# A graph attention kernel: statistics and gain of the output stage moved into layer 2's pass, and the input rows added on POOL

## Chip, cores and metric

The kernel runs on one core of one Trainium2 chip. The metric is device microseconds of one execution. Five engines work side by side, each on its own queue of instructions: TensorE (PE), VectorE (DVE), ScalarE (ACT), GpSimd (POOL) and SyncE (SP, which here only issues transfers). They meet at semaphores.

## What is computed

The input is a graph of 3125 nodes with 256 features each and 53125 edges, sorted by destination. Layer 0 normalises the rows, sums weighted neighbours in both directions and adds the means to x. Then two graph attention layers run over the same edges, layer 1 with 8 heads of 64 features, layer 2 (the output layer) with one head of 256. The stage around the change is the end of layer 2:

```
e = exp(-leaky_relu(s_src[src] + s_dst[dst]))
h_prime = segment_sum(e[:, None] * h[dst], src, num_segments=N)   # 3125 x 256
mu, var = mean(h_prime, axis=-1), var(h_prime, axis=-1)
h_prime = (h_prime - mu) * rsqrt(var + 1e-5) * g_out + beta_out
x = x + elu(h_prime)
```

Everything is float32.

## The kernel before

Nodes are tiled by 128 (T = 25 tiles). Edges were sorted by tile earlier in the kernel, each tile's edges are padded to groups of 256, and a group is two chunks of 128 edges. There are 232 groups, a bound that holds for any graph of this size, so 464 chunks, taken four at a time as 116 quads, numbered 0 to 115. The groups behind the last real edge are padding and belong to the last tile. `tiles_done(groups)` gives how many tiles are complete for sure after so many groups. `FIRST` is the first quad after which one is (103), and `BLOCKS` lists, for each quad from there on, the tiles which that quad is sure to complete: 13 blocks, tile 0 alone and then two tiles each.

One pass over the quads is `attend(o)`, with o = "2" for the output layer; the function stands once for each engine, and all loops are unrolled in Python, four quads a turn. For a quad q:

- POOL issues four gathers (L389, one indirect DMA for 128 rows of the table) into 16 slots; a slot is free again when PE has summed its chunk. Half of the slots lie in `rows_near`, half in `given`.
- ACT makes one-hot matrices (L568, L572), PE transposes them and looks up the source scores (L817, L827).
- DVE adds the two scores when the rows have landed (L1186) and takes leaky relu (L1190), ACT the exponential (L581), DVE the messages (L1199 for layer 2, four instructions), PE the sums of two groups in PSUM (L842, eight matmul records), and DVE adds each to its tile in `work` (L1040).

DVE's order in one turn is: messages of quad q, scores of q + 1, additions of q - 1. Each engine's queue is in program order, so an instruction that waits holds all behind it.

After the pass comes the output stage. DVE takes row statistics of 25 tiles (L1302), then their moments (L918), ACT one square root over all tiles (L652). Then a loop over tiles goes round three engines: DVE subtracts the mean and multiplies by g (L1308), ACT multiplies by 1/std (L657), POOL adds beta (L479), ACT takes relu(-y) and its exponential (L613, L615) and DVE finishes ELU (L1242) and adds x into one of four output slots (L1299). DVE runs six tiles behind itself: `finish(t - 6)` follows the product of tile t. SP writes each output slot to DRAM (L376). The one-hot, message and output buffers share a scratch area.

The blocks of layer 0 (`beside_rows` on DVE, L1144 on) do a like thing to what the change does: statistics of a block's tiles inside a pass.

Of the kernel before, what the change touches and what calls it, by code (L numbers as in the profile page):

```python
# [9 lines left out]
ALU = mybir.AluOpType  # L10
# [5 lines left out]
C = 256  # L16
# [3 lines left out]
HD = HEADS * D  # L20
# [31 lines left out]
def tiles_done(groups):  # L52
    return sum(1 for t in range(T) if (E + (t + 1) * (GROUP - 1)) // GROUP <= groups)
# [3 lines left out]
BLOCKS = [range(tiles_done(2 * q), tiles_done(2 * q + 2)) for q in range(FIRST, QUADS)]  # L57
SUMS0 = 6
assert tiles_done(GROUPS) == T and all(1 <= len(b) <= 2 for b in BLOCKS) and len(BLOCKS) < 16
assert CHUNKS % SLOTS == 0 and CHUNKS <= 512 and P * COLS >= E and FULL < P and COLS % BATCH == 0  # L60
assert SLOT_W <= 12 * HD and T % BLOCK == 0 and all(c % 2 == 0 for c in CUT)

def build(nc, x, src, dst, edge_weight, W_heads, b_heads, a_heads, g_heads, beta_heads,
          W_out, b_out, a_out, g_out, beta_out, out):
    ctx = ExitStack()
    with ctx:
# [37 lines left out]
        square = carve(0, 8, HD)  # L104
        neg_exp = carve(4 * HD, 2, HD)
        final = carve(6 * HD, 4, C)
# [197 lines left out]
        square_used = sem("square_used")  # L304
        scaled = sem("scaled")
        gained = sem("gained")
# [74 lines left out]
        def _(pool):  # L381
# [95 lines left out]
            for t in range(T):  # L477
                pool.wait_ge(scaled, t + 1)
                nc.gpsimd.tensor_tensor(work[:, t, 0:C], work[:, t, 0:C], betao[:, :], ALU.add).then_inc(offset_added, 1)  # L479

        @block.scalar
        def _(act):
# [123 lines left out]

            def elu_exponential(n, slot, y):

                e = neg_exp[:, slot, 0:y.shape[-1]]
                act.wait_ge(offset_added, n + 1)  # L610
                if n >= 2:
                    act.wait_ge(z_done, n - 1)
                nc.scalar.activation(e, y, ACT.Relu, scale=-1.0).then_inc(act_chain, 1)  # L613
                act.wait_ge(act_chain, n + 1)
                nc.scalar.activation(e, e, ACT.Exp, scale=-1.0).then_inc(exp_ready, 1)  # L615
# [34 lines left out]
            attend("2")  # L650
            act.wait_ge(moments_ready, 3 * T)
            nc.scalar.activation(rstd[:, :], mv[:, :, 1], ACT.Sqrt, bias=eps[:, :]).then_inc(std_ready, 1)  # L652
            act.wait_ge(nb_ready, 2 + len(BLOCKS))
            for t in range(T + 2):
                if t < T:
                    act.wait_ge(gained, t + 1)
                    nc.scalar.activation(work[:, t, 0:C], work[:, t, 0:C], ACT.Copy, scale=rstd[:, t:t + 1]).then_inc(scaled, 1)  # L657
                if t >= 2:
                    elu_exponential(t - 2, t % 2, work[:, t - 2, 0:C])

# [212 lines left out]
        def _(dve):  # L873
# [290 lines left out]
            for n in range(4):  # L1164
                beside_rows(QUADS + 2 + n)

            def attend(o):
                heads, width = (HEADS, HD) if o == "1" else (1, C)
# [42 lines left out]
                def turn(i):  # L1211

                    tiles = tile_numbers(mybir.EngineType.DVE, "S", i * (2 * UNROLL) + (TILE_AT - 2), 2 * UNROLL)
                    for u in range(UNROLL):
                        q, static = i * UNROLL + u, isinstance(i, int)
                        messages(q, u)
                        if not static or q + 1 < QUADS:
                            scores(i, i * UNROLL + (u + 1), u + 1)
                        if not static or q >= 1:
                            add_groups(i * UNROLL + (u - 1), u - 1, tiles[2 * u:2 * u + 2])  # L1220

                scores(0, 0, 0)
# [13 lines left out]
            def per_head(a):  # L1236
                return a.rearrange("p (h d) -> p h d", h=HEADS)

            def elu(n, slot, y):

                dve.wait_ge(exp_ready, n + 1)
                return v.scalar_tensor_tensor(out=y, in0=neg_exp[:, slot, 0:y.shape[-1]], scalar=-1.0, in1=y, op0=ALU.add, op1=ALU.max)  # L1242

# [48 lines left out]

            def finish(t):
                y = work[:, t, 0:C]
                elu(t, t % 2, y).then_inc(z_done, 1)
                dve.wait_ge(z_done, t + 1)
                if t >= 4:
                    dve.wait_ge(q_out[t % 4], 16 * (t // 4))
                v.tensor_tensor(final[:, t % 4, :], y, xs[:, t, :], ALU.add).then_inc(final_ready, 1)  # L1299

            for t in range(T):
                v.bn_stats(stats[:, t, :], work[:, t, 0:C]).then_inc(stats_ready, 1)  # L1302
            for t in range(T):
                tile_moments(t, 2 * T)
            dve.wait_ge(moments_ready, 3 * T)
            for t in range(T):

                v.scalar_tensor_tensor(out=work[:, t, 0:C], in0=work[:, t, 0:C], scalar=mv[:, t, 0:1], in1=go[:, :],  # L1308
                                       op0=ALU.subtract, op1=ALU.mult).then_inc(gained, 1)
                if t == 0:  # L1310
                    dve.wait_ge(std_ready, 2 + len(BLOCKS))
                    v.reciprocal(rstd[:, :], rstd[:, :]).then_inc(nb_ready, 1)
                if t >= 6:
                    finish(t - 6)
            for t in range(T - 6, T):
                finish(t)
# [21 lines left out]
```

## Time and profile before

| | us |
|---|---|
| median of 3 executions | 3050.62 |
| lowest, highest | 3050.2, 3058.38 |
| the profiled execution | 3054.22 |
| its span, first to last instruction | 3052.4 |
| DVE, PE, ACT, POOL busy in the span | 2157.3, 2332.0, 1582.3, 1967.1 |

The span is that of the profiled execution; times such as 2996.12 are microseconds from its start. A group line gives engine, source line, operation, output and inputs by tile names, and how many instructions it merges; in a timeline the first two numbers are the start and the length in us, and brackets at the end say how long the engine was idle before and for whom. The table of stretches lists, after the length of each stretch, busy us and count of PE matmuls, PE weight loads, DVE, ACT and POOL, then the granted clock of PE (1.00 would be 2.4 GHz, 0.50 is 1.2 GHz), the share of the transfer engines and GB/s. Shares of the whole span mix five stages with different limits, so the rows below are of single stretches. Layer 2's pass runs from about 2400 to 2996.5, the output stage behind it.

### The profile page before, as it was taken

How to read it: one execution, taken by the hardware profiler on the slowest of the kernel's cores; microseconds unless marked ns; L12 is line 12 of the kernel's file. 1: busy time of each engine (PE TensorE's matmuls, PEld its weight loads, DVE VectorE, ACT ScalarE, POOL GpSimd, SP SyncE). 2: the span in 40 equal slices, each digit the busy share in tenths (PEclk: the TensorE clock that was granted, in tenths of full speed). 3: DMA queues.
4: the chain of work that ended last, by engine and by line, in shares of the span. 5: the costliest groups of instructions: out<-in, count | busy, mean ns of one | idle time of the engine just before them, and what ended most of it. 6: DMA issues, size and time to landing. Idle time of an engine off the chain costs nothing. (4 is left out here: it accounts for less than half of the span.)

```text
span 3052.4 us, 48976 instructions
## 1 busy us (share of the span) xinstructions
PE 2332.0 (76%) x16450; PEld 1796.2 (59%) x16450; DVE 2157.3 (71%) x4448; ACT 1582.3 (52%) x4526; POOL 1967.1 (64%) x2003
## 2 busy tenths in 40 slices
PE   1787699989888899966677888888865677777771
PEld 1677698879887799843344444444434555555551
DVE  9999989988986799832244887888877344343437
ACT  0464467656765676633333555455539455555544
POOL 2000177777777777777773777777756477777772
PEclk7999899989998899955568999999987778777885
DMA  2001011111114322222254777777760233333352
GB/s 64 1 1 44 11 50 50 50 50 50 50 50 47 54 50 50 57 54 52 53 64 119 209 211 205 205 209 211 207 126 19 87 107 106 106 106 106 106 96 56
DMA packets 114891, 270.64 MB, mean 89 GB/s; under 512 B 34543, under 2 KB 51670, under 8 KB 114646
## 3 DMA queue, kind: packets, MB, share of 16 engines
q0 software_dynamic: 89088, 245.53, 32.7%
q1 hardware_dynamic: 25558, 21.98, 2.2%
q8 instruction: 137, 2.24, 0.3%
q14 instruction: 108, 0.88, 0.1%
HBM read 250.96 MB, written 16.42 MB: 88 GB/s over the span
## 5 line engine op out<-in xcount | busy, mean ns | idle before, releaser
L389 POOL DMA_INDIRECT rows_near<-table_a,s_idx_S x464 | 486.4, 1048 | 227.4 <-issue 111.5
L1040 DVE TENSOR_TENSOR work<-work,bank 128x129 f32 (+2 forms) x928 | 390.2, 420 | 288.7 <-PE bank L726 195.1
L389 POOL DMA_INDIRECT rows_near<-table,s_idx_S x464 | 450.0, 970 | 173.4 <-issue 124.3
L389 POOL DMA_INDIRECT rows_near<-table_b,s_idx_D x464 | 465.7, 1004 | 141.4 <-issue 115.2
L389 POOL DMA_INDIRECT given<-table,s_idx_S x464 | 447.2, 964 | 141.3 <-issue 125.2
L726 PE MATMUL bank<-rows_near,oh 128*128 128x129 f32 x1856 | 376.4, 339 | 154.5 <-ACT rows_near L498 122.4
L712 PE MATMUL bank<-scratch 128*128 128x224 bf16 (+1 forms) x2520 | 395.6, 267 | 100.3 <-DVE scratch L1015 78.0
L842 PE MATMUL bank<-scratch,oh 128*128 128x512 f32 x928 | 438.5, 617 | 21.5 <-DVE scratch L1201 21.4
L712 PE MATMUL bank<-rows_near,sort_ring 128*128 128x224 bf16 (+1 forms) x2520 | 395.4, 267 | 50.1 <-DVE sort_ring L1015 29.7
L726 PEld LDWEIGHTS bank<-rows_near,oh 128*128 128x128 f32 x1856 | 291.8, 226 | 226.6 <-ACT rows_near L498 160.8
L581 ACT ACTIVATE e_att<-lrelu 128x32 f32<-128x32 f32 (+1 forms) x232 | 50.4, 217 | 606.9 <-DVE lrelu L1190 606.9
L489 ACT ACTIVATE scratch<-scratch,given 128x128 bf16<-128x128 bf16 x840 | 253.9, 387 | 138.0 <-DVE scratch L1009 138.0
L712 PEld LDWEIGHTS bank<-scratch 128*128 128x128 bf16 x2520 | 245.1, 99 | 119.4 <-issue 69.6
L489 ACT ACTIVATE sort_ring<-sort_ring,given 128x128 bf16<-128x128 bf16 x840 | 253.9, 387 | 101.2 <-DVE sort_ring L1009 101.2
L568 ACT ACTIVATE scratch<-iota_f,s_lo_S 128x128 f32<-128x128 f32 x928 | 293.5, 389 | 18.5 <-PE bank L798 13.9
L498 ACT ACTIVATE rows_near<-rows_near,s_w_D 128x128 f32<-128x128 f32 x464 | 169.5, 396 | 246.6 <-DMA rows_near<-table_b,s_idx_D 246.0
L842 PEld LDWEIGHTS bank<-scratch,oh 128*128 128x128 f32 x928 | 172.2, 196 | 202.1 <-issue 169.0
L498 ACT ACTIVATE rows_near<-rows_near,s_w_S 128x128 f32<-128x128 f32 x464 | 170.2, 395 | 225.5 <-DMA rows_near<-table_a,s_idx_S 224.2
L712 PEld LDWEIGHTS bank<-rows_near,sort_ring 128*128 128x128 bf16 x2520 | 245.2, 99 | 68.7 <-DVE sort_ring L1015 38.1
L827 PEld LDWEIGHTS bank<-sort_ring,scratch 128*128 128x128 bf16 x2784 | 138.3, 98 | 207.3 <-issue 186.2
L713 PE MATMUL bank<-rows_near,sort_ring 128*128 128x224 bf16 (+1 forms) x840 | 223.9, 267 | 0.0
L713 PE MATMUL bank<-scratch 128*128 128x224 bf16 (+1 forms) x840 | 223.8, 266 | 0.0
(201 smaller groups left out, 4410.4 us busy)
## 6 DMA issues: line engine op xcount, KB each, us to landing
rows_near<-table_a,s_idx_S POOLq DMA_INDIRECT x464, 2.6
rows_near<-table_b,s_idx_D POOLq DMA_INDIRECT x464, 2.6
rows_near<-table,s_idx_S POOLq DMA_INDIRECT x464, 3.6
given<-table,s_idx_S POOLq DMA_INDIRECT x464
table<-scratch SPq DMA_DIRECT2D x25, 260.0 KB, 2.1
table<-scratch SPq DMA_DIRECT2D x25, 128.5 KB, 2.9
xs<-in_x SPq DMA_DIRECT2D x1, 3072.0 KB
out_x<-scratch SPq DMA_DIRECT2D x24, 128.0 KB, 1.7
```

The source lines that it names most:

```text
L389: nc.gpsimd.indirect_dma_start(out=to, out_offset=None, in_=table[:, :], in_offset=bass.IndirectOffsetOnAxis(ap=s_idx[order][:, c:c + 1], ...
L489: last = nc.scalar.activation(oh_i2[n % RING][:, j, :], oh_lane[n % RING][:, j, :], ACT.Copy, scale=odd_and_lo[o][:, c:c + 1])
L498: nc.scalar.activation(rows0[:, slot, 0:HALF], rows0[:, slot, 0:HALF], ACT.Copy, scale=s_w[o][:, c:c + 1]).then_inc(rows_scaled, 1)
L568: last = nc.scalar.activation(off_by[:, side + k, :], iota_f[:, 0:P], ACT.Abs, scale=-1.0, bias=s_lo["S"][:, bass.ds(q * QUAD + k, 1)])
L581: nc.scalar.activation(e_att[:, u % 2, 0:QUAD * heads], lrelu[:, u % 2, 0:QUAD * heads], ACT.Exp, scale=-1.0).then_inc(e_ready[o], 1)
L712: nc.tensor.matmul(bank[0][:, at:to], oh_w[n % RING][f][:, j, :], chunks, start=start and f == 0, stop=stop and f == 2)
L713: nc.tensor.matmul(bank[1][:, at:to], oh_i1[n % RING][:, j, :], chunks, start=start, stop=stop)
L726: nc.tensor.matmul(sum0(g), oh[:, slot, :], rows0[:, slot, :], start=(k % GP == 0), stop=(k % GP == GP - 1)).then_inc(chunks_summed, 1)
L827: last = nc.tensor.matmul(bank[2 + u % 2][:, k * heads:(k + 1) * heads], ohT[:, u % 2, k * P:(k + 1) * P], s_parts[:, f, bass.ds(tiles[k / ...
L842: mm = nc.tensor.matmul(bank[4 + u % 2 * 2 + k // GP][:, 0:width], lanes, rows, start=(k % GP == 0), stop=(k % GP == GP - 1))
L1040: v.tensor_add(a, a, psum).then_inc(sum_free[o], 1)
```

## The change

Inside layer 2's pass a new function `beside_sums(q)` stands behind the additions of each quad. For the block of tiles that became complete two quads earlier it takes statistics and moments, and for the block before that it does the subtraction of the mean and the product with g. Three more calls behind the pass do what is left. ACT takes the square root in two parts, tiles 0 to 20 (`EARLY` = 21) and 21 to 24, and no longer multiplies by 1/std. DVE does that together with beta in one instruction, then `finish(t - 3)`, which is now ELU alone. POOL, which added beta, now adds x and writes the output slot, and so has the wait for a free output slot. The buffer of exponentials has four slots in place of two.

```
--- before.py
+++ after.py
@@ -56,6 +56,7 @@
 FIRST = next(q for q in range(QUADS) if tiles_done(2 * q + 2))
 BLOCKS = [range(tiles_done(2 * q), tiles_done(2 * q + 2)) for q in range(FIRST, QUADS)]
 SUMS0 = 6
+EARLY = BLOCKS[-3].stop
 assert tiles_done(GROUPS) == T and all(1 <= len(b) <= 2 for b in BLOCKS) and len(BLOCKS) < 16
 assert CHUNKS % SLOTS == 0 and CHUNKS <= 512 and P * COLS >= E and FULL < P and COLS % BATCH == 0
 assert SLOT_W <= 12 * HD and T % BLOCK == 0 and all(c % 2 == 0 for c in CUT)
@@ -102,7 +103,7 @@
         in_tile = scratch[:, 0:T * COLS // 2].bitcast(BF16).rearrange("p (t c) -> p t c", t=T)
         msg = carve(0, 2 * QUAD, HD)
         square = carve(0, 8, HD)
-        neg_exp = carve(4 * HD, 2, HD)
+        neg_exp = carve(4 * HD, 4, C)
         final = carve(6 * HD, 4, C)
         prep = scratch[:, T * COLS // 2:T * COLS // 2 + 2 * COLS].bitcast(I32)
         ohT = scratch[:, 8 * HD:9 * HD].bitcast(BF16).rearrange("p (a b) -> p a b", a=2)
@@ -302,7 +303,6 @@
         centred = sem("centred")
         squared = sem("squared")
         square_used = sem("square_used")
-        scaled = sem("scaled")
         gained = sem("gained")
         offset_added = sem("offset_added")
         exp_ready = sem("exp_ready")
@@ -475,8 +475,10 @@
             pool.wait_ge(tab_2[1], 16 * (T // 2))
             gather_layer1("2", table_2, W2)
             for t in range(T):
-                pool.wait_ge(scaled, t + 1)
-                nc.gpsimd.tensor_tensor(work[:, t, 0:C], work[:, t, 0:C], betao[:, :], ALU.add).then_inc(offset_added, 1)
+                pool.wait_ge(z_done, t + 1)
+                if t >= 4:
+                    pool.wait_ge(q_out[t % 4], 16 * (t // 4))
+                nc.gpsimd.tensor_tensor(final[:, t % 4, :], work[:, t, 0:C], xs[:, t, :], ALU.add).then_inc(final_ready, 1)
 
         @block.scalar
         def _(act):
@@ -604,14 +606,14 @@
                     turn(i)
                 turn(ROUNDS - 1)
 
-            def elu_exponential(n, slot, y):
-
-                e = neg_exp[:, slot, 0:y.shape[-1]]
-                act.wait_ge(offset_added, n + 1)
-                if n >= 2:
-                    act.wait_ge(z_done, n - 1)
-                nc.scalar.activation(e, y, ACT.Relu, scale=-1.0).then_inc(act_chain, 1)
-                act.wait_ge(act_chain, n + 1)
+            def elu_exponential(t):
+
+                e = neg_exp[:, t % 4, :]
+                act.wait_ge(offset_added, t + 1)
+                if t >= 4:
+                    act.wait_ge(z_done, t - 3)
+                nc.scalar.activation(e, work[:, t, 0:C], ACT.Relu, scale=-1.0).then_inc(act_chain, 1)
+                act.wait_ge(act_chain, t + 1)
                 nc.scalar.activation(e, e, ACT.Exp, scale=-1.0).then_inc(exp_ready, 1)
 
             attend("1")
@@ -648,15 +650,11 @@
                 if n >= 2:
                     head_features(n - 2)
             attend("2")
-            act.wait_ge(moments_ready, 3 * T)
-            nc.scalar.activation(rstd[:, :], mv[:, :, 1], ACT.Sqrt, bias=eps[:, :]).then_inc(std_ready, 1)
-            act.wait_ge(nb_ready, 2 + len(BLOCKS))
-            for t in range(T + 2):
-                if t < T:
-                    act.wait_ge(gained, t + 1)
-                    nc.scalar.activation(work[:, t, 0:C], work[:, t, 0:C], ACT.Copy, scale=rstd[:, t:t + 1]).then_inc(scaled, 1)
-                if t >= 2:
-                    elu_exponential(t - 2, t % 2, work[:, t - 2, 0:C])
+            for a, b in ((0, EARLY), (EARLY, T)):
+                act.wait_ge(moments_ready, 2 * T + b)
+                nc.scalar.activation(rstd[:, a:b], mv[:, a:b, 1], ACT.Sqrt, bias=eps[:, :]).then_inc(std_ready, 1)
+            for t in range(T):
+                elu_exponential(t)
 
         @block.tensor
         def _(pe):
@@ -1164,6 +1162,21 @@
             for n in range(4):
                 beside_rows(QUADS + 2 + n)
 
+            def beside_sums(q):
+
+                n = q - FIRST - 2
+                if 0 <= n - 1 < len(BLOCKS):
+                    for t in BLOCKS[n - 1]:
+                        dve.wait_ge(moments_ready, 2 * T + t + 1)
+                        v.scalar_tensor_tensor(out=work[:, t, 0:C], in0=work[:, t, 0:C], scalar=mv[:, t, 0:1], in1=go[:, :],
+                                               op0=ALU.subtract, op1=ALU.mult).then_inc(gained, 1)
+                if 0 <= n < len(BLOCKS):
+                    dve.wait_ge(sum_free["2"], 4 + 2 * (FIRST + n + 1))
+                    for t in BLOCKS[n]:
+                        v.bn_stats(stats[:, t, :], work[:, t, 0:C]).then_inc(stats_ready, 1)
+                    for t in BLOCKS[n]:
+                        tile_moments(t, 2 * T)
+
             def attend(o):
                 heads, width = (HEADS, HD) if o == "1" else (1, C)
                 acc = work[:, :, 0:width]
@@ -1218,6 +1231,8 @@
                             scores(i, i * UNROLL + (u + 1), u + 1)
                         if not static or q >= 1:
                             add_groups(i * UNROLL + (u - 1), u - 1, tiles[2 * u:2 * u + 2])
+                        if o == "2":
+                            beside_sums(q)
 
                 scores(0, 0, 0)
                 turn(0)
@@ -1235,11 +1250,6 @@
 
             def per_head(a):
                 return a.rearrange("p (h d) -> p h d", h=HEADS)
-
-            def elu(n, slot, y):
-
-                dve.wait_ge(exp_ready, n + 1)
-                return v.scalar_tensor_tensor(out=y, in0=neg_exp[:, slot, 0:y.shape[-1]], scalar=-1.0, in1=y, op0=ALU.add, op1=ALU.max)
 
             def head_means(n):
 
@@ -1291,28 +1301,22 @@
 
 
             def finish(t):
+                dve.wait_ge(exp_ready, t + 1)
                 y = work[:, t, 0:C]
-                elu(t, t % 2, y).then_inc(z_done, 1)
-                dve.wait_ge(z_done, t + 1)
-                if t >= 4:
-                    dve.wait_ge(q_out[t % 4], 16 * (t // 4))
-                v.tensor_tensor(final[:, t % 4, :], y, xs[:, t, :], ALU.add).then_inc(final_ready, 1)
-
-            for t in range(T):
-                v.bn_stats(stats[:, t, :], work[:, t, 0:C]).then_inc(stats_ready, 1)
-            for t in range(T):
-                tile_moments(t, 2 * T)
-            dve.wait_ge(moments_ready, 3 * T)
-            for t in range(T):
-
-                v.scalar_tensor_tensor(out=work[:, t, 0:C], in0=work[:, t, 0:C], scalar=mv[:, t, 0:1], in1=go[:, :],
-                                       op0=ALU.subtract, op1=ALU.mult).then_inc(gained, 1)
-                if t == 0:
-                    dve.wait_ge(std_ready, 2 + len(BLOCKS))
-                    v.reciprocal(rstd[:, :], rstd[:, :]).then_inc(nb_ready, 1)
-                if t >= 6:
-                    finish(t - 6)
-            for t in range(T - 6, T):
+                v.scalar_tensor_tensor(out=y, in0=neg_exp[:, t % 4, :], scalar=-1.0, in1=y, op0=ALU.add, op1=ALU.max).then_inc(z_done, 1)
+
+            for q in range(QUADS, QUADS + 3):
+                beside_sums(q)
+            for n, a, b in ((0, 0, EARLY), (1, EARLY, T)):
+                dve.wait_ge(std_ready, 2 + len(BLOCKS) + n)
+                link(v.reciprocal(rstd[:, a:b], rstd[:, a:b]))
+                for t in range(a, b):
+                    dve.wait_ge(gained, t + 1)
+                    y = work[:, t, 0:C]
+                    v.scalar_tensor_tensor(out=y, in0=y, scalar=rstd[:, t:t + 1], in1=betao[:, :], op0=ALU.mult, op1=ALU.add).then_inc(offset_added, 1)
+                    if t >= 3:
+                        finish(t - 3)
+            for t in range(T - 3, T):
                 finish(t)
```

## Rows read from the trace of the kernel before

**Rows 1.** Chain of waits, the end of it: start, us, what.

```profile
2976.03 14.30 DMA given<-table,s_idx_S
...
2992.23 3.77 PE bank L842 x8
...
2996.12 0.43 DVE work L1040
2996.58 8.27 DVE stats L1302 x25
```

**Rows 2.** Stretches of the output stage: window, length, then each engine's busy us.

```profile
2996.54:3006.50 9.96, 0.00 (x0) 0.00 (x0) 9.93 (x51) 0.00 (x0) 0.00 (x0) 0.50 0.00 0
3006.50:3047.70 41.20, 0.00 (x0) 0.00 (x0) 40.08 (x77) 32.16 (x77) 19.71 (x25) 0.50 0.21 74
```

**Rows 3.** Waits in 2925 to 2997: who, for whom, total us, times, longest.

```profile
DVE score L1186 <- DMA given<-table,s_idx_S: 24.1, 6, 5.1
```

**Rows 4.** Timeline of the last tiles, and SP's last wait.

```profile
3045.67 0.42 DVE L1299 TENSOR_TENSOR scratch<-work,xs 128x256 f32<-128x256 f32 x1
...
3046.01 0.42 DVE L1242 SCALAR_TENSOR_TENSOR work<-scratch,work 128x256 f32<-128x256 f32 x1
...
3047.26 0.42 DVE L1299 TENSOR_TENSOR scratch<-work,xs 128x256 f32<-128x256 f32 x1
...
SPq L66 <- DMA out_x<-scratch: 3.1, 1, 3.1
```

**Rows 5.** Timeline of one steady tile of the output loop, DVE and POOL.

```profile
3037.01 0.47 DVE L1308 SCALAR_TENSOR_TENSOR work<-work,mv,sort_ring 128x256 f32<-128x256 f32 x1
...
3037.40 0.41 DVE L1242 SCALAR_TENSOR_TENSOR work<-scratch,work 128x256 f32<-128x256 f32 x1
3037.65 0.75 POOL L479 TENSOR_TENSOR work<-work,sort_ring 128x256 f32<-128x256 f32 x1 [0.85 <-ACT work L657]
...
3038.60 0.47 DVE L1308 SCALAR_TENSOR_TENSOR work<-work,mv,sort_ring 128x256 f32<-128x256 f32 x1
```

**Rows 6.** Timeline of the loop's start, both engines' queues full.

```profile
3008.25 0.95 DVE L1308 SCALAR_TENSOR_TENSOR work<-work,mv,sort_ring 128x256 f32<-128x256 f32 x1
...
3008.88 0.90 POOL L479 TENSOR_TENSOR work<-work,sort_ring 128x256 f32<-128x256 f32 x1
...
3009.74 0.90 POOL L479 TENSOR_TENSOR work<-work,sort_ring 128x256 f32<-128x256 f32 x1
3009.98 0.94 DVE L1308 SCALAR_TENSOR_TENSOR work<-work,mv,sort_ring 128x256 f32<-128x256 f32 x1
```

**Rows 7.** Timeline of DVE in layer 0: two statistics, two moments, then the next.

```profile
1600.15 0.75 DVE L913 BATCH_NORM_STATS2 stats<-xs 128x6 f32<-128x256 f32 x2
...
1601.04 0.66 DVE L1032 TENSOR_TENSOR oh<-iota_f,s_lo_D 128x512 f32<-128x512 f32 x1
```

**Rows 8.** Timeline of the pass: one quad's sums, then the first reuse of its slots.

```profile
2947.15 1.97 PE L842 MATMUL bank<-rows_near,scratch 128*128 128x256 f32 x8
...
2957.28 0.95 POOL L389 DMA_INDIRECT rows_near<-table,s_idx_S  x1 [0.30 <-issue]
```

**Rows 9.** Timeline of the last turn: the messages of quad 115.

```profile
2991.80 0.87 DVE L1199 TENSOR_SCALAR scratch<-oh,e_att 128x128 f32<-128x128 f32 x4
```

**Rows 10.** Layer 1's messages (ns), gathers beside them, gathers of layer 2 (total, mean ns).

```profile
L1201 DVE TENSOR_TENSOR scratch<-rows_near,e_att x232: 677/684/729, 1670.4 to 2259.4; 128x512 f32<-128x512 f32 x116
...
L389 POOL DMA_INDIRECT given<-table,s_idx_S x157 | 153.3, 976 | 47.8 <-issue 45.1 <-DVE scratch L1201 2.7
...
L389 POOL DMA_INDIRECT given<-table,s_idx_S x216 | 205.5, 951 | 65.8 <-issue 52.7 <-PE bank L842 13.1
```

**Rows 11.** Timeline: the reciprocal; first relu, table load, first ELU.

```profile
3006.94 0.31 DVE L1312 RECIPROCAL rstd<-rstd 128x25 f32<-128x25 f32 x1
...
3008.95 0.42 ACT L613 ACTIVATE scratch<-work 128x256 f32<-128x256 f32 x1 [0.36 <-POOL work L479]
...
3011.13 0.42 DVE L1242 SCALAR_TENSOR_TENSOR work<-scratch,work 128x256 f32<-128x256 f32 x1 [0.21 <-ACT scratch L615]
```

## The prediction

> **What bounds the kernel now.** I read the page first (section 2: PE is empty in the last slices), then the chain of waits from its end, then the timeline of the last 60 us, then the table of stretches for the same 60 us. The chain shows two different tails [rows 1]. The pass of layer 2 ends on a transfer, not on an engine: the last gather is issued at 2976.03 and lands 14.30 us later, then come the scores, the messages and the last sums on PE, and the last addition starts at 2996.12. From there DVE alone carries the chain: statistics of 25 tiles from 2996.58. The table of stretches says the same as shares [rows 2]: DVE is busy 9.93 of 9.96 us with ACT and POOL at nothing, and after it 40.08 of 41.20 us with ACT at 32 and POOL at 20. So the output stage, 2996.54 (last addition over) to 3047.68 (last row of the output ready), is 51.1 us of DVE work, while inside the pass DVE stands still: in the last 72 us of it the waits of DVE for gathered rows come to 24.1 us for one half of the buffers alone, the longest 5.1 [rows 3]. That is the trade the change makes.
>
> **What a DVE instruction costs here.** The reported length of a 128x256 instruction (0.42 to 0.48 us) overlaps the next one; the spacing of starts is the cost. Undisturbed, from the addition at 3045.67 to the ELU at 3046.01 it is 0.34 [rows 4], and I take 0.345. With a wait that has just been answered it is 0.39 (3037.01 to 3037.40 [rows 5]). Beside POOL additions it is more: with both engines' queues full, a DVE instruction starts at 3008.25 and the next but one at 3009.98, with two POOL additions (3008.88, 3009.74) in that time, so 0.865 for one of each [rows 6]; a POOL addition takes 0.865 - 0.345 = 0.52 of DVE's time. The steady tile of the old loop checks this: 0.39 + 0.345 + 0.345 for its three DVE instructions and 0.52 for its POOL addition give 1.60, and the tile takes 3038.60 - 3037.01 = 1.59 [rows 5].
>
> **The change, part A: the work put into the pass.** After the additions of quad q - 1 each of quads 105 to 115 now carries the product with g of two tiles (2 x 0.345), two statistics and two moments. The same four instructions in layer 0 run from 1600.15 to the next instruction at 1601.04, 0.89 us [rows 7]. Together 1.58 us a quad, ten times and a smaller first one. New waits: for sum_free, whose count 4 + 2(q - 1) has been passed before the wait is reached, since the additions of quad q - 1 make it 4 + 2q; and for moments, made one quad before. Neither should hold anything. What is queued behind them on DVE is the messages of quad q + 1, and behind those PE's sums and POOL's gathers into the freed slots. In all turns but the last two things hide a delay of the messages: DVE waits up to 5.1 us for rows before the scores [rows 3], and PE's sums of a quad start at 2947.15 and take 1.97, while the gathers that reuse their slots start only at 2957.28, 8.2 us after the sums are over [rows 8]. So there I cost A at nothing; if that cover were gone it would be 1.58 us a quad. In the last turn there is no cover: the scores of quad 115 have landed, the messages start at 2991.80 directly behind an addition [rows 9], and the block now comes between. The end of the pass moves by **+1.6** us. The block of the next quad lies beside PE's 3.75 us of sums. Bounds of the term: 1.8 with the reported 0.47 for each product, and -0.2 if PE ran its last eight matmuls in the 1.97 us of [rows 8] instead of the 3.77 of [rows 1]. I keep 1.6: PE's granted clock is low around it and a later start gives no reason for a better one.
>
> Do the new instructions disturb the gathers? Layer 1's messages also have two SBUF inputs and run beside the same gathers: they take 677/684/729 ns (least, median, most), never a gather's length more, and the gathers beside them 976 ns against 951 in layer 2 [rows 10]. That is 0.03 us a gather, within a pass that waits for landings; I take nothing.
>
> **Part B: from the last addition to the first instruction of the output loop.** Before: 2996.54 to 3006.54, 10.0 us. After: what is left over is products of blocks 10, 11 and 12 (6 x 0.345 = 2.1), statistics of four tiles (2 x 0.89 = 1.8) and a reciprocal with a wait for its own end (0.3, [rows 11]): 4.2 us. **-5.8** us. The square root for the first 21 tiles needs only moments made inside the pass, so it is ready; the one for the last four runs on ACT beside the last products. With the reported lengths in place of the spacings B is 4.9.
>
> **Part C: the output loop.** Before: 3006.54 to 3047.68, 41.1 us. The new one has two DVE instructions a tile (scale with offset, ELU) and POOL's addition of x, behind DVE rather than ahead of it. Start: the first product with 1/std (0.42), handover (0.07), then ACT's relu, table load and exponential, which from relu to ELU took 3008.95 to 3011.13, 2.18 [rows 11]: 2.7 us to the first ELU, with three more tiles scaled meanwhile. Then 21 pairs. DVE alone would need 0.69 to 0.78 of it, ACT less than the 0.795 a tile that [rows 4] show (two tiles from 3045.67 to 3047.26), but POOL's addition reads two SBUF operands beside DVE instructions that do so too, as in [rows 6]: 2 x 0.345 + 0.52 = 1.21 at least, 2 x 0.39 + 0.52 = 1.30 if each wait costs its 0.045. I take 1.25: one of the two waits, that for the products, is long answered. 21 x 1.25 = 26.3. The second reciprocal 0.3. ELUs of the last four tiles with POOL's additions between, 3 x 0.87 = 2.6, and the last ELU, handover and POOL addition, 0.42 + 0.1 + 0.75 = 1.3. Sum 33.2: **-7.9** us. A slot of the output buffer is reused after four tiles, at least 3.5 us; in [rows 4] the tiles were 0.8 us apart and no wait for the transfer shows, so that wait costs nothing. The end behind the last tile is the transfer (its landing waited for 3.1 us [rows 4]) and stays, now behind POOL.
>
> The lock itself deserves a second look, because the reported length of POOL's addition is 0.75 [rows 5], not 0.52. The Trainium skill, page "SBUF — State Buffer", section "Who interferes with whom", says that a DVE instruction with two SBUF inputs and a GpSimd instruction that reads SBUF share a port, and that the later one fully blocks until the first is over; the 0.865 of [rows 6] agrees that they exclude each other. Taken with POOL's whole reported length that rule would give -6.6 us in place of the -12.1 below, the first rival. The Trainium skill, page "Perfetto Trace Analysis", section "GPSIMD Engine Instruction", calls such lengths unreliable and wants spacings; by that rule the sum is the one below.
>
> **Sum.** +1.6 - 5.8 - 7.9 = **-12.1 us**. The profiled execution took 3054.22 (span 3052.4 and 1.8 around it), so 3042.1 for such a one. The median of the runs, 3050.62, lies 3.6 below that execution, which I carry over: **3038.5 us**. The bounds of the terms (A -0.2 to 1.8, B 4.2 to 4.9, the pair 1.21 to 1.30) make -14.7 to -10.4, that is 3036 to 3040.5.
>
> **Rivals.** (1) POOL holds DVE for its whole 0.75: the pair is 1.43 to 1.53, take 1.48; 21 x 0.23 + 3 x 0.22 = 5.5 more, -6.6, **3044.0**. For it: the reported length, and POOL now stands behind DVE so that who comes first changes. Against it: the steady tile of [rows 5] would then be 1.83, and is 1.59. (2) The two don't collide, since POOL falls into gaps: 0.795 a tile, 21 x 0.455 + 1 = 10.5 less, **3028**. Against it: DVE leaves no gaps in such a loop. (3) The slower side: the block in the pass lies in series in each quad, and each product is blocked by a whole gather instruction of 0.95 us. Then a quad costs 1.6 + 1.9 = 3.5, eleven of them 38.5, against B + C = -13.7: +24.8, **3075**. It turns to slower by 0.3% from (13.7 + 9.2)/11 = 2.1 us a quad. In series but unblocked, 17.6 - 13.7 = +3.9, **3054.5**. Against both: the idle time and the slack of [rows 3, 8] and the even 0.68 of [rows 10]. (4) The change doesn't do what it says: tiles are not complete where their block comes, the wait for the sums holds, and the statistics end up behind the pass as before; only C is saved, -7.9, **3042.7**. The counts worked out in A speak against it.
>
> **How the numbers follow.** About 0.3% (9.2 us) is what a measurement of this kernel can tell from no change. Forecast 0.75; rival 1 0.12; rival 2 0.04; rival 3 0.04 blocked and 0.03 in series; rival 4 0.02. Faster by over 9.2 us: 0.93 of the forecast's share (a few of its cases fall short) and rival 2, 0.74. Within: the rest of the forecast, rivals 1 and 4 and the serial case, 0.21. Slower 0.05: the blocked case, and a little for an unseen one. The range takes the forecast's own 3036 to 3040.5, some us to either side for a sum of 60 instructions taken from spacings and a median of few runs, and most of rival 1: 3032 to 3045; what is left out (rival 2, rival 3, a piece of rival 1) is under 0.2.
>
> **What the profile after would show.** A: between the additions of a quad and its messages two products, two statistics, two moments, 1.6 us, in quads 105 to 115; gathers at an unchanged pace; the last addition at about 2998.1. B: first scaled tile 4.2 us behind it. C: ELU to ELU 1.25 us in the steady part, POOL additions at the same spacing, an ACT with gaps. The prediction is wrong if ELUs are 1.43 or more apart (rival 1) or 0.8 (rival 2), if waits for gathers before the scores vanish and quads get longer (rival 3), if DVE waits for sums inside the block (rival 4), or if POOL waits for output slots.

## The result

The changed kernel takes 3043.38 us in the median of 16 executions (3035.42 to 3047.88), the kernel before 3050.41 (16 executions, 3045.16 to 3058.38). The ratio is 0.9975, interval 0.9968 to 0.9982: 5.5 to 9.8 us faster, and less than the 12.1 forecast. The forecast time was 3038.5 in a range of 3032 to 3045. In the profiled executions the spans are 3052.4 and 3041.8, 10.6 apart; the next paragraphs show that 2 of these are not the change's.

The table of stretches of the changed kernel, for the part behind the last addition. Columns as in [rows 2]: window, its length, busy us of PE, of its weight loads, DVE, ACT and POOL, clock, transfer share, GB/s.

```profile
2996.38:3000.86 4.48, 0.00 (x0) 0.00 (x0) 4.41 (x17) 0.30 (x1) 0.00 (x0) 0.50 0.00 0
3000.86:3033.95 33.09, 0.00 (x0) 0.00 (x0) 30.77 (x51) 21.34 (x51) 21.97 (x25) 0.50 0.26 92
3033.95:3041.80 7.85, 0.00 (x0) 0.00 (x0) 0.00 (x0) 0.00 (x0) 0.00 (x1) 0.50 0.07 24
```

The first answers to the first of [rows 2] (10.0 us before), the second to its second (41.1 us before). The third is new: from the end of POOL's last addition no engine is busy for 7.85 us. Before, the last row of the output was ready at 3047.68 and the span ended 4.72 us later. That is 3.1 us given back at the very end.

The same reading for the two kernels, from the first score of quad 115 (the landing of the last gather) on, by the starts and ends in the timelines:

| stretch, us | before | after | change | forecast |
|---|---|---|---|---|
| A: score of quad 115 to the end of the last addition | 6.09 | 8.12 | +2.0 | +1.6 |
| B: to the first instruction of the output loop | 10.0 | 4.5 | -5.5 | -5.8 |
| C: to the last row of the output ready | 41.1 | 33.1 | -8.0 | -7.9 |
| D: to the end of the span | 4.7 | 7.8 | +3.1 | 0 |
| sum | 61.95 | 53.54 | **-8.4** | -12.1 |

What lies ahead of this stretch differs by another 2.2 us between the two profiled executions (first score of quad 115 at 2990.45 and at 2988.26). The pass itself began 4.7 us earlier in the changed kernel's execution, with the same code up to there, and the first 419 of its gathers, before any quad that the change touches, took 2 us longer. So executions differ by some us ahead of the change, which is why I compare stretches of the tail as well as medians.

### The profile page after: what moved, and what is told of

The parts are those of the page before. It is cut to its first block and busy times, and to the rows that moved or that the text cites. A ratio compares the mean times of both kernels' runs of the same rounds, so it can differ in the third digit from the quotient of the medians.

```text
span 3041.8 us, 48953 instructions
## 1 busy us (share of the span) xinstructions
PE 2344.4 (77%) x16450; PEld 1798.8 (59%) x16450; DVE 2160.6 (71%) x4449; ACT 1572.7 (52%) x4502; POOL 1963.7 (65%) x2003
## 5 line engine op out<-in xcount | busy, mean ns | idle before, releaser
L710 PE MATMUL bank<-rows_near,sort_ring 128*128 128x224 bf16 (+1 forms) x2520 | 394.2, 266 | 52.2 <-DVE sort_ring L1013 29.8
L825 PE MATMUL bank<-sort_ring,scratch 128*128 x2784 | 162.9, 169 | 79.9 <-ACT scratch L579 71.7
```

Source lines behind the costliest of these rows:

```text
L710: nc.tensor.matmul(bank[0][:, at:to], oh_w[n % RING][f][:, j, :], chunks, start=start and f == 0, stop=stop and f == 2)
L825: last = nc.tensor.matmul(bank[2 + u % 2][:, k * heads:(k + 1) * heads], ohT[:, u % 2, k * P:(k + 1) * P], s_parts[:, f, bass.ds(tiles[k / ...
```

## Where the stretches come from

**A.** The score of quad 115 in the kernel before, then the last turn of the pass in the changed kernel, timeline of DVE with PE's sums between:

```profile
2990.45 0.16 DVE L1186 TENSOR_TENSOR score<-bank,given 128x4 f32<-128x4 f32 x1 [4.21 <-DMA given<-table,s_idx_S]
...
2988.26 0.16 DVE L1199 TENSOR_TENSOR score<-bank,given 128x4 f32<-128x4 f32 x1 [2.53 <-DMA given<-table,s_idx_S]
...
2989.61 0.88 DVE L1171 SCALAR_TENSOR_TENSOR work<-work,mv,sort_ring 128x256 f32<-128x256 f32 x2
2990.40 0.75 DVE L1176 BATCH_NORM_STATS2 stats<-work 128x6 f32<-128x256 f32 x2
2991.06 0.30 DVE L916 BATCH_NORM_AGGREGATE mv<-stats 128x2 f32<-128x6 f32 x2
2991.28 0.84 DVE L1212 TENSOR_SCALAR scratch<-oh,e_att 128x128 f32<-128x128 f32 x4
2991.68 3.75 PE L840 MATMUL bank<-given,scratch 128*128 128x256 f32 x8 [3.42 <-DVE scratch L1212]
...
2993.00 0.88 DVE L1171 SCALAR_TENSOR_TENSOR work<-work,mv,sort_ring 128x256 f32<-128x256 f32 x2
...
2995.33 0.42 DVE L1038 TENSOR_TENSOR work<-work,bank 128x256 f32 x1 [0.57 <-issue]
2995.96 0.42 DVE L1038 TENSOR_TENSOR work<-work,bank 128x256 f32 x1 [0.21 <-DVE work L1038]
```

The block of quad 114 runs from 2989.61 to 2991.28, between the additions and the messages, as forecast. It takes 1.67 us where 1.58 was worked out: its two products take 0.79 (2989.61 to 2990.40) and not 0.69. The messages thus start 3.02 us behind the score, against 1.35 before (2990.45 to 2991.80 [rows 9]). PE's eight matmuls again take 3.75. The other 0.36 us: the block of quad 115 was to lie beside PE, but DVE comes out of it so late that its own queue, with a load of tile numbers into registers (the 0.57 us marked issue), and no longer PE, times the last two additions. The last one starts 0.53 us after PE is through (2995.43 to 2995.96), against 0.14 before, and neither waits for PE any more.

**B.** The first block behind the last addition:

```profile
2996.42 0.88 DVE L1171 SCALAR_TENSOR_TENSOR work<-work,mv,sort_ring 128x256 f32<-128x256 f32 x2
2997.22 0.75 DVE L1176 BATCH_NORM_STATS2 stats<-work 128x6 f32<-128x256 f32 x2
2997.88 0.30 DVE L916 BATCH_NORM_AGGREGATE mv<-stats 128x2 f32<-128x6 f32 x2
2998.10 0.86 DVE L1171 SCALAR_TENSOR_TENSOR work<-work,mv,sort_ring 128x256 f32<-128x256 f32 x2
```

Two statistics and two moments take 0.88 us (2997.22 to 2998.10), as counted. Two products take 0.80 and not 0.69, a little under 0.4 each; over six products that is the 0.3 by which B falls short.

**C.** Two tiles of the loop, once it is steady:

```profile
3009.35 0.94 DVE L1306 SCALAR_TENSOR_TENSOR work<-scratch,work 128x256 f32<-128x256 f32 x1
...
3010.22 0.47 DVE L1316 SCALAR_TENSOR_TENSOR work<-work,rstd,sort_ring 128x256 f32<-128x256 f32 x1
3010.37 0.90 POOL L481 TENSOR_TENSOR scratch<-work,xs 128x256 f32<-128x256 f32 x1 [0.36 <-DVE work L1306]
3010.61 0.94 DVE L1306 SCALAR_TENSOR_TENSOR work<-scratch,work 128x256 f32<-128x256 f32 x1
...
3011.48 0.47 DVE L1316 SCALAR_TENSOR_TENSOR work<-work,rstd,sort_ring 128x256 f32<-128x256 f32 x1
3011.63 0.90 POOL L481 TENSOR_TENSOR scratch<-work,xs 128x256 f32<-128x256 f32 x1 [0.36 <-DVE work L1306]
```

A tile takes 3011.63 - 3010.37 = 1.26 us (forecast 1.25). Of DVE's two instructions the ELU, which starts while POOL adds, is drawn out to 0.94 where it takes 0.41 in [rows 5]. From its start at 3010.61 the next instruction comes 0.87 us later, as in [rows 6] (0.865).

**D.** What each queue does at the close: the drain, its last instruction in the block ahead of the semaphores at which all queues meet, in ns, on POOL and on SP. The changed kernel, then the kernel before:

```profile
L67 POOLq DRAIN  x1: 8832/8832/8832, 3032.7 to 3032.7; - x1
L67 SPq DRAIN  x1: 7/7/7, 3038.2 to 3038.2; - x1
...
L66 POOLq DRAIN  x1: 8577/8577/8577, 3043.6 to 3043.6; - x1
L66 SPq DRAIN  x1: 7/7/7, 3052.0 to 3052.0; - x1
```

and SP's last waits (total us, times, longest), in the same order:

```profile
SPq L67 <- PEq L67: 3.5, 1, 3.5
SPq L67 <- DMA out_x<-scratch: 3.0, 1, 3.0
...
SPq L66 <- PEq L66: 0.4, 1, 0.4
```

POOL's queue starts its drain while the last addition still runs, and the drain is over 7.6 us after that addition's end: 3032.7 + 8.8 = 3041.5 against 3033.95. In the kernel before it was over at 3043.6 + 8.6 = 3052.2, two tenths after SP's own (3052.0): the two ended together, since POOL's last instruction (beta) lay 3.1 us ahead of the last output row. The transfers of the changed kernel take no longer (SP waits 3.0 us for the last one, 3.1 in [rows 4]), and SP is through at 3038.2. Then it waits 3.5 us for the other queues to meet it; the view names PE's queue there, and e1 and e2 below show that it was POOL's drain that came last. By making POOL write the last rows, the change put a drain that used to be covered behind everything else.

## Experiments

The readings of all kernels stand together here. "Score to add" is A, "to last row" is B and C together, "row to end" is D, "POOL to end" is the end of POOL's last instruction other than a gather to the end of the span. The ratios are to the kernel before on the same chip, with intervals; e5, e6 and e7 ran on a chip that is slower as a whole (the kernel before takes 3474 us there, and 3049 to 3057 on the chips of all the others). The expectations of e1, e5 and e7 speak of 8.5 us behind the last output row of the changed kernel; the table, which counts from the end of the last addition, has 7.85 for it.

| kernel | score to add | to last row | row to end | POOL to end | score to end | ratio |
|---|---|---|---|---|---|---|
| before | 6.09 | 51.14 | 4.72 | 7.83 | 61.95 | |
| changed | 8.12 | 37.57 | 7.85 | 7.85 | 53.54 | 0.9975 (0.9968 to 0.9982) |
| e1: last five x on DVE | 8.14 | 36.38 | 4.72 | 8.41 | 49.24 | 0.9954 (0.9940 to 0.9967) |
| e2: before, POOL late | 6.09 | 51.13 | 7.94 | 7.78 | 65.16 | 1.0018 (1.0009 to 1.0027) |
| e3: all x on DVE | 8.13 | 32.57 | 4.64 | none | 45.34 | 0.9939 (0.9926 to 0.9953) |
| e4: before, statistics in pass | 6.95 | 43.03 | 4.69 | 7.81 | 54.67 | 0.9982 (0.9973 to 0.9992) |
| e5: POOL only writes (slower chip) | 8.13 | 26.10 | 7.84 | 7.84 | 42.07 | 0.9958 (0.9947 to 0.9970) |
| e6: statistics thrice (slower chip) | 11.82 | 37.55 | 7.84 | 7.84 | 57.21 | 1.0009 (0.9998 to 1.0021) |
| e7: changed again (slower chip) | 8.13 | 37.57 | 7.84 | 7.84 | 53.54 | 0.9969 (0.9953 to 0.9985) |
| e8: thrice, not in the last turns | 8.13 | 37.56 | 7.82 | 7.82 | 53.51 | 0.9977 (0.9967 to 0.9988) |
| e9: all x on DVE again | 8.12 | 32.57 | 4.71 | none | 45.40 | 0.9951 (0.9937 to 0.9965) |
| e10: changed, third time | 8.13 | 37.55 | 7.81 | 7.81 | 53.49 | 0.9973 (0.9965 to 0.9982) |

**Is it the drain or the transfers?** First, take POOL out of the last five tiles of the changed kernel:

```
-            for t in range(T):
+            for t in range(T - 5):
                 pool.wait_ge(z_done, t + 1)
+            def add_x(t):          # on DVE, for t >= T - 5, one tile behind the ELU
+                dve.wait_ge(z_done, t + 1)
+                dve.wait_ge(q_out[t % 4], 16 * (t // 4))
+                v.tensor_tensor(final[:, t % 4, :], work[:, t, 0:C], xs[:, t, :], ALU.add).then_inc(final_dve, 1)
```

> The changed kernel, but DVE adds x for the last five tiles, POOL for the first twenty. Theory 1: the end of the kernel is set by POOL's closing drain, which in the changed kernel lasts 8.8 us from POOL's last addition, against 4.7 us of SP's own end; with POOL out five tiles earlier the time from the last output row to the end of the span falls from 8.5 to 4.7 us, and with the last tiles at 0.8 us instead of 1.26 the whole is 4 to 5 us shorter than the changed kernel. Rival: the longer end comes from output transfers that are closer together; then it stays at 8.5 us and only about 1 us is gained.

The row to end fell back to 4.72 us, and POOL's drain now ends half a us ahead of SP's:

```profile
L68 POOLq DRAIN  x1: 8547/8547/8547, 3036.0 to 3036.0; - x1
L68 SPq DRAIN  x1: 7/7/7, 3045.1 to 3045.1; - x1
```

The tail is 4.3 us shorter than the changed kernel's. That fits theory 1 and not the rival. The other way round, in the kernel before:

```
+            pool.wait_ge(final_ready, T)
+            nc.gpsimd.memset(pad_at[:, :], 0.0)
```

> The kernel before, with one tiny memset on POOL that waits for the last output tile. Theory 1 (POOL's drain sets the end): the time from the last output row to the end grows from 4.7 to about 8.3 us, the kernel is 3.5 to 4 us slower than before. Rival (transfers set it): no change, within 1 us.

One memset of one column, which nobody waits for, costs 3.2 us in the tail; the interval of the ratio is 2.8 to 8.3 us:

```profile
L66 POOLq DRAIN  x1: 7712/7712/7712, 3050.1 to 3050.1; - x1
L66 SPq DRAIN  x1: 7/7/7, 3054.4 to 3054.4; - x1
```

SP is through 4.3 us behind the last row in both kernels (3054.4 here, 3052.0 before), so the transfers are not the cause. In the nine executions of the table whose end POOL sets or shares, POOL to end is 7.78 to 7.85 us, whatever that last instruction was (addition or memset) and on the slower chip too. It is not a fixed price, though. Where the gathers are POOL's last work (e3, then e9), the traces have

```profile
L68 POOLq DRAIN  x1: 24483/24483/24483, 2979.9 to 2979.9; - x1
...
L68 POOLq DRAIN  x1: 23060/23060/23060, 2970.2 to 2970.2; - x1
```

and the drain is over 18.6 and 17.0 us after the last gather instruction, in both 3.7 us after the start of the score of quad 115, which waits for the last landing (3000.66 and 2989.60). So it looks as if the drain also waits for POOL's own transfers. What it waits for inside was not tried.

**What POOL's addition costs DVE.** All additions of x on DVE (the lines of e1 with T - 5 replaced by 0, so that POOL has nothing after its gathers):

> The changed kernel with all additions of x on DVE, three DVE instructions a tile, POOL idle after its gathers. If a POOL addition takes 0.52 us from DVE (the port of the prediction), a tile takes about 1.1 us instead of 1.26, the loop is 3.3 us shorter, and with the drain out of the way 7 us are gained on the changed kernel, 14 to 16 us on the one before. Rival: the two engines don't exclude each other and POOL's addition is cheap for DVE; then a third DVE instruction lengthens a tile to about 1.6 us, the loop grows by 8 us, and the kernel is 4 us slower than the changed one.

```profile
3012.39 0.41 DVE L1319 TENSOR_TENSOR scratch<-work,xs 128x256 f32<-128x256 f32 x1
...
3012.73 0.47 DVE L1329 SCALAR_TENSOR_TENSOR work<-work,rstd,sort_ring 128x256 f32<-128x256 f32 x1
3013.12 0.41 DVE L1311 SCALAR_TENSOR_TENSOR work<-scratch,work 128x256 f32<-128x256 f32 x1
...
3013.46 0.41 DVE L1319 TENSOR_TENSOR scratch<-work,xs 128x256 f32<-128x256 f32 x1
```

This is the timeline of its second run, e9. Three DVE instructions a tile take 3013.46 - 3012.39 = 1.07 us, less than the 1.26 of two with POOL beside them. The tail is 8.2 us shorter than the changed kernel's: 3.2 from D and 5.0 from the loop. The loop's share is more than the 3.3 expected; the spacing explains 4.8 (25 tiles at 0.19). The other side of the same question, with POOL's instruction kept in its place but reading nothing:

```
-                nc.gpsimd.tensor_tensor(final[:, t % 4, :], work[:, t, 0:C], xs[:, t, :], ALU.add).then_inc(final_ready, 1)
+                nc.gpsimd.memset(final[:, t % 4, :], 1.0).then_inc(final_ready, 1)
```

> The changed kernel, but POOL only writes a constant into the output slot (memset) where it added x; x is left out of the output. If it is POOL's reading beside DVE's two-operand instructions that costs DVE 0.52 us a tile, DVE goes at its own pace, 0.79 us a tile instead of 1.26, the loop shrinks from 32.4 to about 22 us, and the 8.5 us behind the last tile stay, since POOL is still last. Rival: what costs is any POOL instruction of that length beside DVE, or the waits in the loop; then the tile stays at 1.1 us or more.

```profile
3429.75 0.42 DVE L1306 SCALAR_TENSOR_TENSOR work<-scratch,work 128x256 f32<-128x256 f32 x1
...
3430.24 0.31 POOL L481 MEMSET scratch<- 128x256 f32 x1 [0.44 <-DVE work L1306]
...
3430.51 0.42 DVE L1306 SCALAR_TENSOR_TENSOR work<-scratch,work 128x256 f32<-128x256 f32 x1
```

This kernel leaves x out of the output. A tile takes 0.76 us, and no DVE instruction is drawn out. The chip is not the reason: on the same one e7's stretch to the last row is 37.57 us, and e5's 26.10. So the whole 0.50 us between 0.76 and 1.26 goes with POOL's addition (0.53 with the 0.73 that e9's three instructions less one leave for two), near the 0.52 that the spacings of [rows 6] gave and far from the 0.75 of its reported length [rows 5]. The memset is also shorter, so this run doesn't separate reading from length by itself; that the ELU beside it stays at 0.42, not drawn out at all, speaks for the reading. POOL to end is 7.84, as in e7 beside it.

**One part alone.** In the kernel before, only statistics and moments go into the pass:

```
+                    for t in BLOCKS[n]:
+                        v.bn_stats(stats[:, t, :], work[:, t, 0:C]).then_inc(stats_ready, 1)
+                    for t in BLOCKS[n]:
+                        tile_moments(t, 2 * T)      # in beside_sums(q), behind the additions
...
-            for t in range(T):
-                v.bn_stats(stats[:, t, :], work[:, t, 0:C]).then_inc(stats_ready, 1)
```

> The kernel before, with the statistics and moments alone moved into the pass (0.89 us a quad); product and output loop as before. If the pass hides them but for its last turn: the last addition 0.9 us later, 8.2 us less behind it, together 7.3 us faster than before, and the time from the last output row to the end still 4.7 us. Rival: each of the eleven quads pays its 0.9 us; then 9.8 - 8.2 = 1.6 us slower than before.

The tail is 61.95 - 54.67 = 7.28 us shorter, A is +0.86. So this part alone is worth nearly as much as the whole change in the tail (8.4), because the rest gains 4.3 in A to C and loses 3.2 in D. The ratio's interval (2.4 to 8.3 us) holds the 7.3, and its middle of 5.5 lies below.

**Does the pass hide DVE's work?** Each statistics instruction of the in-pass blocks done three times:

```
+                    if q < QUADS:
+                        for t in BLOCKS[n]:
+                            link(v.bn_stats(stats[:, t, :], work[:, t, 0:C]))
+                            link(v.bn_stats(stats[:, t, :], work[:, t, 0:C]))
```

> The changed kernel with each statistics instruction of the in-pass blocks done three times, each repeat waited for: 1.6 to 1.8 us more on DVE in each of the quads 105 to 115. If the pass hides DVE's work but for the last turn, the last 45 gathers are issued at the pace of the changed kernel (56.7 to 56.8 us) and only the stretch from the last landing to the last addition grows, from 8.1 to about 9.8 us: 1.7 us slower than the changed kernel. Rival: every quad pays; then the last 45 gathers take some 15 us more and the kernel is 17 us slower than the changed one.

> The changed kernel once more, for a comparison with its variants on one chip and for a second trace. If its tail is steady from execution to execution, the stretch from the first score of quad 115 to the end of the span is 53.5 us again within 0.5, with 8.5 us behind the last output row, and the last 45 gathers take 56.7 to 56.8 us; the rest of the span may differ by some us, since that part of the code is the same in all kernels.

Both ran on the slower chip. e7's tail came as expected (53.54), but its last 45 gathers took 67.7 us and not 56.7: the pass goes slower there. Neither theory held for e6. Score to add grew by 3.7 us, not 1.7: the block of the last turn costs as well, since DVE's queue and not PE times the last additions. And the last scores don't wait for a landing any more:

```profile
3412.53 0.84 DVE L1216 TENSOR_SCALAR scratch<-oh,e_att 128x128 f32<-128x128 f32 x4
3413.29 0.15 DVE L1203 TENSOR_TENSOR score<-bank,given 128x4 f32<-128x4 f32 x1
```

(in the changed kernel DVE stood idle for 2.53 us there). From the last gather's issue to that score it is 12.9 us against 10.1 in e7. The last 45 gathers took 69.3 us, against 67.7 in e7 and 66.3 in e5, whose pass is the same as e7's. 3.7, 2.8 and 1.6 make 8.1, and the medians, 3476.4 and 3468.0, are 8.3 apart; but the 1.6 is hardly more than the 1.4 between e7 and e5. With 1.7 us more, the last quads' cover is used up on this chip. Its pass has another limit as well. POOL's waits for PE's sums, on whose end a slot comes free, over the last gathers of e7 (3342 to 3411, slower chip) and of e10 (2914 to 2970, see below), total us, times, longest:

```profile
POOL rows_near L389 <- PE bank L840: 4.7, 4, 1.8
POOL given L389 <- PE bank L840: 1.3, 1, 1.3
...
POOL given L389 <- PE bank L840: 1.2, 4, 0.3
POOL rows_near L389 <- PE bank L840: 0.9, 3, 0.3
```

On the slower chip gathers are held by the sums, for up to 1.8 us (another 7.7 us in four waits stands there as "remote", which no run here explains); on the other none is held longer than the 0.3 that stands between any two gathers. The next test spares quads 114 and 115 (`if q < QUADS - 2`), and ran on another chip than e6:

> As the kernel with statistics done three times, but quads 114 and 115 do them once, so that the extra 1.7 us of DVE work lie in quads 105 to 113 alone, 15 us in all. If those quads hide DVE's work: the stretch from the first score of quad 115 to the end is that of the changed kernel, 53.5 us, the last 45 gathers are issued within 1 us of its pace on the same chip, and the kernel equals the changed one within 2 us. Rival: a part of each quad's extra work reaches the gathers; the last 45 gathers are longer by up to 15 us, and the kernel slower by as much.

> The changed kernel again, as the partner of the two kernels beside it: 53.5 us from the first score of quad 115 to the end, 7.8 us from the end of POOL's last addition to the end of the span, and 7 to 8 us faster than the kernel before in the median.

```profile
2967.26 0.16 DVE L1203 TENSOR_TENSOR score<-bank,given 128x4 f32<-128x4 f32 x1
...
2974.16 0.16 DVE L1203 TENSOR_TENSOR score<-bank,rows_near 128x4 f32<-128x4 f32 x1 [1.18 <-DMA rows_near<-table,s_idx_S]
```

Some scores find their rows there, others still wait, and by quad 115 the delay has been made up. The tail is 53.51 us, like 53.49 for e10 beside it; the last 45 gathers take 56.81 and 56.60 us, the medians are 3042.72 and 3041.48. Fifteen us of extra DVE work in nine quads cost nothing that can be told from zero. Since e6 and e8 differ in the chip too, they don't tell how much of e6's loss comes from the last two quads and how much from the slower chip, where the slack of [rows 8] is partly gone; neither kernel was run on the other's chip. Over all kernels on the faster chips, the last 45 gathers took 56.42, 56.31 and 56.26 us without products in the pass (before, e2, e4) and 56.60 to 56.81 with them (changed, e1, e3, e8, e9, e10). That is three executions against six without overlap: the products seem to reach the gathers a little, about 0.4 us in all, and statistics alone don't.

**The version that beats both.**

> The changed kernel with all additions of x on DVE once more, beside the changed kernel itself on one chip. If the tail is what differs, 53.5 against 45.3 us from the first score of quad 115 to the end, it is 8 us faster than the changed kernel and 14 to 18 us faster than the one before. Rival: the earlier 18.7 us were luck of its executions and only half of the 8 us shows.

The tail is 45.40 us, 8.1 less than e10's beside it. The medians are 3034.98 for e9, 3041.48 for the changed kernel and 3049.26 for the one before: 6.5 us between e9 and the changed kernel (e9's slowest execution, 3037.55, is below e10's fastest, 3037.95), and 0.9951 (0.9937 to 0.9965) to the one before, 10.7 to 19.2 us. Statistics and product in the pass, additions of x on DVE, and POOL idle after its gathers is the fastest of these kernels.

## Why the prediction came out as it did

**The time lay in the range and the direction held, but the saving was forecast too large by 5 us** (3038.5 against 3043.4). The sum was wrong by one term.

- **D, nothing: wrong, +3.1.** The step said that the end behind the last tile is the transfer "and stays, now behind POOL". I had read SP's wait of 3.1 us [rows 4] as what ended the span and never looked at the other queues' closing instructions. POOL's drain ended there too, 0.2 us later than SP, and its cover was that POOL's last instruction lay 3.1 us ahead of the last row. e1 and e2 show it from both sides. The change moved the last instruction from one engine to another, and the price of an engine being last belonged in the sum.
- **A, +1.6: right in mechanism, 2.0 measured.** Blocks of 1.67 us, hidden in all quads but the last turn, as e8 shows. Of the 0.4 too little, 0.1 is the products' spacing and the rest the claim that the block of quad 115 lies beside PE's sums. It does, but fills them and more, so that DVE times the end of the pass. The reason for not taking the lower bound held (PE's sums took 3.75 us again); the upper bound of 1.8 was too low, as it left out the wait of the additions behind that block. A second small miss, 0.4 us for the gathers beside the products, was costed at nothing from [rows 10].
- **B, -5.8: -5.5 measured.** 4.5 us in place of 4.2. Statistics ran at the spacing used, the products at 0.39 to 0.40 where 0.345 was taken.
- **C, -7.9: -8.0 measured.** A tile at 1.26 (1.25), first ELU after 2.69 us (2.7). Working with the spacing of starts and not with reported lengths made this term right. Moving the addition to POOL takes 0.50 us from DVE to save the 0.34 of a DVE instruction, so this part of the change loses, as e3 and e9 show. The Trainium skill, page "SBUF — State Buffer", section "Who interferes with whom", says that a DVE instruction with two SBUF inputs contends with a GpSimd instruction that reads SBUF and not with one that only writes it. The traces agree: the ELU takes 0.94 us beside POOL's addition and 0.42 beside the memset of e5.
- **The rivals.** Rival 1 (1.48 a tile) and rival 2 (0.8) fell with the 1.26. Rival 3 (in series in each quad) fell with e8, though e6, on the slower chip, overran its cover. Rival 4 fell: no wait for sums stands inside a block. Nor did POOL wait for output slots: its 22 waits in the loop are all for DVE's ELU. The mechanism that took the gain away, an engine's closing drain, was in none of them.
- **The median.** The tail's -8.4 and the gathers' +0.4 make -8.0; the medians give -7.0 (5.5 to 9.8), and e10 -7.8. This agrees. The bounds of the forecast's own terms, -14.7 to -10.4, missed all of these (their upper end adds up to -10.1, which is the 3040.5 of the text). The wider range held the time thanks to rival 1, whose mechanism was not what happened: that it holds 3043.4 is luck.

## To carry to other kernels

Before moving the last instructions of a kernel to another engine, read when each engine's closing drain ends and which of them has been hidden by coming early. Where two engines exclude each other, an instruction moved from one to the other must cost less than it saves: compare spacings of starts with and without the neighbour, not reported lengths. Work put into an engine's idle time inside a pass was free here until the turn in which the pass ends; there it is paid in full, and beside the last wait it fits only as far as that wait is long. How deep that idle time is can differ from chip to chip (e7 and e10 are one kernel on two), so read it on the one that counts.

## What the runs showed of the hardware

POOL's queue needs 7.6 us from the end of its last instruction to the end of its closing drain, and the span ends 7.8 us after that instruction (7.78 to 7.85 in nine executions), with the last gather issued from POOL some 40 us or more earlier. Where POOL did nothing after its gathers (e3, e9), the drain was over 18.6 and 17.0 us after the last gather instruction, 3.7 us after the score that waited for the last landing; that is before the output loop began, and it cost nothing. For DVE the same drain took 0.46 us in the kernel before, most of it beside DVE's last instruction, and SP's took 0.007.

An addition of two 128x256 tiles on POOL took 0.50 to 0.53 us from DVE instructions with two inputs beside it, less than its reported 0.75 to 0.90; a memset of the same size drew none of them out.
